# The middle 28 heads of an attention kernel on a hardware loop of two turns, on three of five engines

## The reference, cut to what matters

```
xn  = layernorm(x)
q,k,v = xn @ Wq.T + bq, ...      # 16 heads of 16 channels, 2 sequences: 32 heads
out = softmax(q k^T / 4) v       # 4096 x 4096 scores for each of the 32 heads
y   = x + out @ Wo.T + bo + experts(xn)    # 8 gated experts, routed
```

## Time and profile before

| | us |
|---|---|
| median of 3 runs | 6686.24 (6683.4 to 6695.13) |
| the profiled execution | 6707.44 |
| its span, first to last instruction | 6705.6 |
| TensorE busy | 6530.0 (97%) |
| VectorE busy | 5739.6 (86%) |
| ScalarE busy | 4984.7 (74%) |
| GpSimd busy | 517.9 (8%) |

### The profile page before, as it was taken

How to read it: one execution, slowest core, us unless ns; L and a number is a source line. 1 busy time by engine, 2 the same in 40 slices (tenths; PEclk the granted TensorE clock), 3 DMA queues, 4 the chain that set the end, 5 groups by cost and what they waited for, 6 DMA issues and landing times. The chain is left out here.

```text
span 6705.6 us, 142426 instructions
## 1 busy us (share of the span) xinstructions
PE 6530.0 (97%) x57168; PEld 3115.6 (46%) x57168; DVE 5739.6 (86%) x6099; ACT 4984.7 (74%) x9109; POOL 517.9 (8%) x543
## 2 busy tenths in 40 slices
PE   7999999979999999999999999999999999999996
PEld 6888888833333333333333333333333333333334
DVE  4555545489999999999999999999999999999982
ACT  3333333328888888888888888888888888888884
POOL 2222222200000000000000000000000000000000
PEclk9999999969999999999999999999999999999998
DMA  2111111121111111111111111111111111111104
GB/s 93 45 45 45 45 45 45 38 37 27 33 33 29 29 29 29 30 29 29 29 29 29 29 29 29 29 29 29 33 32 32 30 32 34 33 29 29 29 10 158
DMA packets 239500, 247.25 MB, mean 37 GB/s; under 512 B 154537, under 2 KB 199337, under 8 KB 232489
## 3 DMA queue, kind: packets, MB, share of 16 engines
q1 hardware_dynamic: 226656, 202.89, 13.6%
q0 software_dynamic: 12176, 35.14, 2.1%
HBM read 159.26 MB, written 76.58 MB: 35 GB/s over the span
## 5 line engine op out<-in xcount | busy, mean ns | idle before, releaser
L918 DVE TENSOR_REDUCE mx<-sc 128x1 f32<-128x1024 f32 x4096 | 5004.6, 1224 | 130.4 <-PE sc L792 60.2
L901 ACT ACTIVATE pr<-st 128x512 f32<-128x512 f32 x8120 | 4412.9, 597 | 644.6 <-PE st L806 447.6
L819 PE MATMUL pv<-pr,vst 128*32 128x256 f32 x32768 | 2611.8, 391 | 18.3 <-ACT oT L888 10.4
L806 PE MATMUL st<-experts 50*128 50x512 f32 x8120 | 2035.4, 497 | 17.0 <-ACT pr L901 6.4
L792 PE MATMUL sc<-experts 48*128 48x512 f32 x8192 | 1672.1, 403 | 36.4 <-DVE mx L918 27.7
L806 PEld LDWEIGHTS st<-experts 50*128 50x128 f32 x8120 | 761.1, 183 | 1691.6 <-ACT pr L901 1637.5
L819 PEld LDWEIGHTS pv<-pr,vst 128*32 128x32 f32 x32768 | 647.9, 108 | 1532.1 <-issue 771.2
L792 PEld LDWEIGHTS sc<-experts 48*128 48x128 f32 x8192 | 794.1, 190 | 76.7 <-DVE mx L918 64.9
L433 ACT ACTIVATE gated<-gate 128x512 f32<-128x512 f32 x256 | 152.2, 599 | 629.8 <-PE up L76 629.6
L603 DVE TENSOR_TENSOR hraw<-gated,up 128x512 f32<-128x512 f32 x256 | 173.3, 686 | 429.5 <-ACT gated L433 426.6
L76 PE MATMUL gate<-xT,experts 128*128 128x512 f32 x1536 | 406.9, 401 | 10.5 <-issue 10.5
(11 more groups left out here) (103 smaller groups left out, 1315.1 us busy)
## 6 DMA issues: line engine op xcount, KB each, us to landing
experts<-parts_d SPq DMA_DIRECT2D x372, 256.0 KB, 4.3
parts_d<-part SPq DMA_DIRECT2D x64, 512.0 KB, 3.0
x_in<-in_L_attn_hidden_states SPq DMA_DIRECT2D x16, 512.0 KB, 4.5
v_d<-v_sb SPq DMA_DIRECT2D x32, 256.0 KB, 2.2
vst<-v_d SPq DMA_DIRECT2D x128, 64.0 KB, 2.2
sums_d<-oT SPq DMA_DIRECT2D x256, 32.0 KB
whole<-sums_d POOLq DMA_DIRECT2D x32, 256.0 KB, 3.0
recs<-rden_d POOLq DMA_DIRECT2D x32, 256.0 KB, 5.6
```

The costliest lines, as they stand in the source:

```text
L806: nc.tensor.matmul(score_bank(x + grp, final), kr[par][r0:r0 + ROWSM, kb * P:(kb + 1) * P], qr[par][r0:r0 + ROWSM, q0:q0 + GT], start=True ...
L819: last = nc.tensor.matmul(pv[VC * j:VC * (j + 1), cols], vst[par][:, kb, :], pr[:, (QSUB * kb + j) % PRING, cols], start=(kb == 0 and half ...
L901: nc.scalar.activation(pr[:, (QSUB * kb + j) % PRING, :], score_bank(x, last and q == PER - 1), ACT.Exp).then_inc(st_read, 1)
L918: nc.vector.reduce_max(mx[par][:, u // MAXU, u % MAXU:u % MAXU + 1], sc[g % 2][:, :], AX.X).then_inc(sc_read, 1)
```

## The change

SyncE's stream stays written out in full; only its `body` takes other arguments. TensorE, ScalarE and VectorE now run the first two heads written out, then a `Fori` loop of two turns with 14 heads each, then the last two heads written out. Inside the loop the number of the head is a register, so each wait there compares with a value that register instructions work out first. GpSimd's part of the attention is not touched. No matmul, activation, reduction or transfer is added, removed or reordered.

```diff
-        PERH = 4
-        PER = 2 * PERH
-        LAST = HEADS // PERH - 1
+        ENDH = 2
+        TURNS = 2
+        BODYH = (HEADS - 2 * ENDH) // TURNS
 ...
         def in_turn(body):
-            for i in range(LAST + 1):
-                body(i, i == 0, i == LAST)
+            body(0, ENDH, True, False)
+            for i in range(TURNS):
+                body(ENDH + i * BODYH, BODYH, False, False)
+            body(HEADS - ENDH, ENDH, False, True)
+
+        def rolled(engine, body):
+
+            body(0, ENDH, True, False)
+            with engine.Fori(0, TURNS) as i:
+                body(ENDH + i * BODYH, BODYH, False, False)
+            body(HEADS - ENDH, ENDH, False, True)
 ...  # in the bodies of SP, PE, ACT and DVE alike:
-            def body(i, first, last):
-                for q in range(PER):
-                    s, n, par, hf = PER * i + q, PERH * i + q // 2, q // 2 % RING, q % 2
-                    ending = last and q // 2 == PERH - 1
+            def body(h0, heads, first, last):
+                for q in range(2 * heads):
+                    s, n, par, hf = 2 * h0 + q, h0 + q // 2, q // 2 % RING, q % 2
+                    ending = last and q // 2 == heads - 1
 ...
-            in_turn(body)
+            rolled(pe, body)        # SP keeps in_turn(body)
 ...
-            in_turn(body)
+            rolled(act, body)
 ...
-                            inverted(PERH * i + q // 2 - 1)
-
-            in_turn(body)
+                            inverted(h0 + q // 2 - 1)
+
+            rolled(dve, body)
```

More of the change, by code:

```diff
@@ L855, in body @@
                             to = q + 1 + u // UNITS
-                            if not (last and to >= PER):
+                            if not (last and to >= 2 * heads):
                                 max_unit(UNITS * (s + 1) + u, u % UNITS, to // 2 % RING, to % 2)
@@ L891, in _, with body @@
             rows_kept()
-            def body(i, first, last):
-                for q in range(PER):
-                    s, hf = PER * i + q, q % 2
+            def body(h0, heads, first, last):
+                for q in range(2 * heads):
+                    s, hf = 2 * h0 + q, q % 2
                     for kb in range(KB):
@@ L898, in body @@
                         for j in range(QSUB):
-                            x = slot_of(kb, j, last and q == PER - 1)
+                            x = slot_of(kb, j, last and q == 2 * heads - 1)
                             act.wait_ge(st_full, s * SLOTS + x + 2)
-                            nc.scalar.activation(pr[:, (QSUB * kb + j) % PRING, :], score_bank(x, last and q == PER - 1), ACT.Exp).then_inc(st_read, 1)
+                            nc.scalar.activation(pr[:, (QSUB * kb + j) % PRING, :], score_bank(x, last and q == 2 * heads - 1), ACT.Exp).then_inc(st_read, 1)
                         if kb == 0 and not (first and q == 0):
                             sums_kept(s - 1)
-                        if kb == ROWS_AT and not (last and q == PER - 1):
+                        if kb == ROWS_AT and not (last and q == 2 * heads - 1):
                             act.wait_ge(rows_in, (s + 1) * ROW_MOVES * DMA)
@@ L945, in _, with body @@
                 max_unit(UNITS + u, u, 1)
-            def body(i, first, last):
-                for q in range(PER):
-                    s = PER * i + q
+            def body(h0, heads, first, last):
+                for q in range(2 * heads):
+                    s = 2 * h0 + q
                     for kb in range(KB):
@@ L953, in body @@
                             to = q + 1 + u // UNITS
-                            if not (last and to >= PER):
+                            if not (last and to >= 2 * heads):
                                 max_unit(UNITS * (s + 1) + u, u % UNITS, to % 2)
-                            if last and q == PER - 1:
+                            if last and q == 2 * heads - 1:
                                 continue
```

## The result

The changed kernel took 6703.24 us (median of 20 runs, 6693.06 to 6711.37) against 6691.51 for the kernel before beside it (20 runs, 6683.01 to 6703.41). The ratio is 1.0013, 95% interval 1.0007 to 1.0019 (the quotient of the two medians is 1.0018): within 0.2%, on the slower side. The forecast was 6674.4. The profiled execution took 6708.88 us, its span 6707.1, against 6707.4 and 6705.6 before.

What follows compares the result with a forecast made beforehand. Steps alternate between a TensorE-ScalarE cycle and TensorE's own 1.240 us. Waits -10.6, late exponentials -3.7, back edge +2.5 sum to -11.8 us, giving 6674.4 with 21.2 carried over; own range 6668 to 6681, with rivals 6663 to 6702.

Steps and rivals of the forecast that it cites:

- the back edge: One jump back on each of three engines: pauses of 3.7 us that overlap, +2.5 us in all (bounds 0 and 11.1).
- the 21.2 us: Timed median lies 21.2 us below the profiled span of 6705.6; the same difference turned 6695.6 into the forecast 6674.4.
- the waits: ScalarE's first exponential per key block loses its standalone wait in the loop: lag 0.10 to 0.04, -0.20 us a half.
- L799's waits: TensorE's standalone waits before score pairs, two a half, go in the loop: -0.07 us a half.
- the wait for oT: TensorE's matmul behind the copy to oT: its late wait falls on a register operation, +0.08 us a half.
- register operations: Five a key block on TensorE and ScalarE, two on VectorE; they lie beside the engines' work, costed at nothing.
- late exponentials: Rare first exponentials 0.28 us late on ScalarE, some 13 events, vanish with the standalone wait: -3.7 us.
- the third rival: Register operations before the first exponential run late: lag 0.12, +41 us, total 6730 us; chance 20%.
- the first: Rival: the standalone wait before the first exponential stays in the loop, so only the jump is left: 6688.7 us; chance 12%.
- The second rival: The three engines' pauses at the jump back follow one another, costing 11.1 us: 6683.0 us; chance 8%.
- TensorE's floor: TensorE's own work limits a score-pair step to at least 1.240 us, so loop steps would average 1.240.
- the mean of 1.224: Sign against the forecast: a mean step of 1.224 us, a VectorE reduction's time, would show TensorE's floor was misplaced.

Runs made afterwards that it cites:

- e12: The changed kernel a third time, on the third chip: 6713.71 us against 6713.28 for the kernel before, ratio 0.9997.
- e9: The kernel before against itself, a control with a second trace, on the third chip: 6713.68 us against 6713.28, ratio 1.0003.
- e5: The changed kernel again, with a second trace, on the second chip: 6677.99 us against 6704.48 for the kernel before, ratio 0.9963.
- e14: The changed kernel, a fourth trace, on the fourth chip: 6710.06 us against 6715.35 for the kernel before, ratio 0.9996.
- e6: The changed kernel with only ScalarE in the loop, TensorE and VectorE written out: 6701.84 us against 6704.48 for the kernel before, ratio 1.0001.
- e8: The changed kernel with only VectorE in the loop, the other two written out: 6711.04 us against 6704.48 for the kernel before, ratio 1.0009.

## Why the prediction was wrong

The forecast was -11.8 us, and the timed runs moved by +11.7. Two terms of the sum failed: the back edge, priced by its pause alone, and the 21.2 us carried over from the profiled execution to the timed runs. The first is shown by runs; that the second explains the rest is in part an inference.

**Right: the waits.** The first exponential's lag fell to 0.04, L799's waits went, and the ordinary half fell from 80.285 to 80.12, 0.17 where 0.19 was worked out. The written-out halves and those of the loop in one execution show the same: 80.27 and 80.11 in e12 and with one turn. In the result's own trace the written-out ones were 79.90, which the last part of this section takes up. One turn and the exchange on ScalarE show the gain without a jump: 0.9986 and 0.9968. The exchange gains though it has no register, which confirms the reason given: what counts is whether the late wait sits on the exponential or on an instruction of its own before it.

**Right: the wait for oT.** It costs what was said.

Timeline of the changed kernel, the copy to oT of half 30 and the matmuls behind it, as in the earlier trace rows.

```profile
3971.48 0.60 ACT L897 ACTIVATE oT<-pv 128x512 f32<-128x512 f32 x1
...
3971.56 0.40 PE L801 MATMUL sc<-experts 48*128 48x512 f32 x2
3972.22 0.64 PE L828 MATMUL pv<-pr,vst 128*32 128x256 f32 x8 [0.26 <-ACT oT L897]
```

The matmul starts 0.66 after the `sc` pair instead of 0.59, and 0.14 after the copy's end instead of 0.05.

**Right: register operations and late exponentials.** TensorE and ScalarE issue some thousands of register operations more, and the steps are 1.24, with a lag of 0.03 to 0.04. That refutes the third rival, and with the 256 semaphore instructions the first. Of the late first exponentials, 14 in the first trace, none is left in the loop, and two copies to oT are late instead: -3.3 of the -3.7.

**Wrong: the back edge, +2.5 us.** It measured 9.8, 12.3, 16.7 and 19.9 in four executions and 13.7 in the mean of six with seven turns, in three of the four beyond the bound of 11.1. The step was half right. Each engine pauses 3 to 4 us, and the pauses do overlap. The second rival had the three pauses one after the other, and falls too, though its 11.1 us are nearer to the cost than the 2.5 forecast.

By source line, sequencers of the changed kernel: the branch and the register write at the top of the body.

```profile
L679 PEldq FUSED_REGOPS  x2: 84/86/88, 1807.6 to 4051.4; - x2
L679 ACTq FUSED_REGOPS  x2: 84/88/93, 1808.0 to 4051.6; - x2
L679 DVEq FUSED_REGOPS  x2: 111/111/111, 1808.4 to 4052.0; - x2
...
L679 PEldq COMPARE_BRANCH  x2: 79/1818/3558, 4047.8 to 6297.9; - x2
...
L679 ACTq COMPARE_BRANCH  x2: 40/42/45, 4048.3 to 6298.4; - x2
...
L679 DVEq COMPARE_BRANCH  x2: 55/64/74, 4048.6 to 6298.7; - x2
```

All three resume between 4051.4 and 4052.0. The prediction looked for 3.7 us in three branches. TensorE's branch has 3.56; ScalarE's and VectorE's have 0.04 and 0.07, and their pauses of 3.2 and 3.3 us lie between the branch and the next instruction. The short VectorE branch of the earlier trace rows was thus no evidence for a short pause. The Trainium skill (Runtime: NRT & Kernel Launch, Instruction fetch mechanics) says that a taken branch to a place outside the loaded pages waits for the fetch, on whichever engine. The traces agree in that all three pause at the jump, and with the hint ScalarE's and VectorE's pauses shrink to 0.4 and 0.5 us and TensorE's branch to 387 ns. Alone in a loop, ScalarE pauses 2.3 us and VectorE 2.7.

What was not priced comes next.

Timeline of the changed kernel, TensorE at the jump.

```profile
4048.29 0.64 PE L828 MATMUL pv<-pr,vst 128*32 128x256 f32 x8
...
4051.75 0.72 PE L815 MATMUL st<-experts 50*128 50x512 f32 x2 [2.82 <-issue]
...
4053.84 0.79 PE L815 MATMUL st<-experts 50*128 50x512 f32 x2
```

Its stretches of 17 us before, in and after the low clock (columns as above).

```profile
4030.00:4047.00 17.00, 16.85 (x161) 6.14 (x161) 16.08 (x17) 14.61 (x29) 0.00 (x0) 1.00 0.01 4
4052.00:4069.00 17.00, 17.00 (x98) 5.31 (x96) 9.40 (x8) 9.27 (x17) 0.54 (x1) 0.50 0.21 43
4070.00:4087.00 17.00, 17.00 (x172) 6.27 (x164) 16.81 (x14) 14.85 (x29) 0.00 (x0) 1.00 0.31 63
```

TensorE stands 2.82 us, as foreseen. Then it runs 17 us at 1.2 GHz and does in them 98 matmuls instead of 161 to 172: 7 us lost beside the 2.8. The front of the attention had already shown such a thing, a low clock that outlasts the idle time (in the first trace TensorE was busy for 10.0 of the 12.0 us from 1471 to 1483, still at 1.2 GHz), and it was not taken over to the jump. With 13.7 in place of 2.5 the prediction's own sum is -10.6 - 3.7 + 13.7 = -0.6 us: no change, as the third and the fourth chip measured (0.9997, 0.9996). The result's timed runs moved by +11.7. Of this, 1.4 is the difference of the two profiled executions and 10.3 comes with the next step. In the profiled executions the gains were larger than forecast (-9.1 - 6.7 - 3.3), the jump took 9.8, and the low clock at the start of the attention added 10.8 by half 3, for which the prediction had no term. It varies from execution to execution in both kernels (106 to 133 us before, 106 to 130 changed), so it is not shown to come from the change.

**Wrong: the profiled execution as the measure of the timed ones.** The 21.2 us between the two were carried over as a constant. They are not one: over 20 runs each they are 15.9 for the kernel before and 5.6 for the changed one. The same program runs at more than one pace. An `sc` matmul takes 397 or 387 ns; in halves of 80.11 nearly all take 397 and the step is 1.240, in halves of 79.45 four in five take 387 and the step is 1.227. So 1.240 was not TensorE's floor, though the mean of 1.224 that the prediction named for this case was not reached either.

Groups by line and form of the changed kernel, 2196 to 2276 us and then 2276 to 2356.

```profile
L801 PE MATMUL sc<-experts 48*128 48x512 f32 x128 | 25.6, 397 | 0.0
...
L801 PE MATMUL sc<-experts 48*128 48x512 f32 x130 | 25.5, 389 | 0.0
```

The kernel before has two as well: 394.9 ns on average from 1800 to 6200 us in its first trace, with halves of 80.285, and 391.2 on the third chip, with 79.91.

Timeline of the kernel before on the third chip (e9), two copies to oT.

```profile
3488.95 0.60 ACT L888 ACTIVATE oT<-pv 128x512 f32<-128x512 f32 x1
...
3568.85 0.60 ACT L888 ACTIVATE oT<-pv 128x512 f32<-128x512 f32 x1
```

At equal pace the waits are therefore worth 80.285 - 80.11 = 0.17 a half at the long one, and 79.91 - 79.45 = 0.46 at the short one. The second is seen within e5 and e14 too, 79.9 written out and 79.45 in the loop. But the two parts of a program need not keep the same pace: in the result's trace the written-out halves in front were 79.90 and most of the loop's 80.12, and in e6 it was 79.9 beside 80.07 and 80.11. With VectorE's loop (e8) all were 80.08, a third value.

For the changed kernel the difference is 80.11 - 79.45 = 0.66 a half, 36 us in 55 halves. Its medians of 6678.0 and 6713.7 lie 35.7 apart, on two chips on which the medians of the kernel before are 8.8 apart, and with jumps of 12.3 and 19.9; that the two numbers are so near is chance. The direction and the size fit timed runs that were all at the one pace there and at the other here, and in e14 the profiled execution was at the short pace and 33 us below the median of its set. But only profiled executions have traces, so for the timed ones it is an inference. For the result: before's profiled 6707.4 lay outside all of its 20 timed runs there, 6683 to 6703, so its timed runs probably had halves nearer to 79.91 than to 80.285, and against those 80.12 is no gain. The one execution traced with 79.91 (e9) took 6694.3, which agrees. What selects the pace stays open.

## What to carry to other kernels

Where two waits stand before an instruction on the critical cycle, put the one that is truly late where it sits on the instruction itself (in these written-out programs that is the one written first): on ScalarE, or on ScalarE and TensorE, this was worth 0.3% to 0.4% on three chips without any loop. The traces at hand (80.03 to 80.10 a half against 79.91) show no gain where the kernel before runs at its short pace. Price a jump back not by its pause but by the pause and by what TensorE's clock does after it, and look for the pause behind the branch as well as in it. Before a forecast of a few tenths of a per cent, compare the profiled execution's time with the timed ones: where it lies outside them, its steps need not be theirs.

## What the runs showed of the hardware

- After an idle stretch of TensorE of 2.6 to 3.2 us at a jump its clock was low for 14 to 41 us, in eleven jumps of eleven. After 1.15 us (VectorE's loop) it fell too, for 20.5, and after 1.45 us (behind the exit of the loop with the hint) for 13.7; after 1.41 us (ScalarE's loop) it did not. The length of the idle stretch alone doesn't decide.
- The same `sc` matmul takes 387 or 397 ns, and the mix of the two holds for halves on end: nearly all 397, or four in five 387. With both exchanges the halves repeat to 10 ns, 80.03, on two chips.
- At the start of the attention the low clock lasted 102 to 133 us in different executions. It was 130 and not 106 in the changed kernel's profiled one, which put its first copy to oT some 10 us later. The kernel before had 133 in another (e9).
